# Expert down products of a mixture-of-experts block on one Trainium2 core: three float32r products of halves instead of one float32 product

## The chip, the cores and the metric

The kernel runs on 1 core of one Trainium2 chip. The metric is the device time of one launch in microseconds (us). Lower is better.

## The reference

The input `x` (2 sequences of 512 tokens, 256 wide) is normalised, and two branches are added to it: 16 heads of causal attention, and a block with a second attention (16 query and 4 key heads, rotary) that is followed by a mixture of 32 experts. The part that the change touches is the last product of an expert, `hmid` times `wed`:

```
probs = jax.nn.softmax(router_logits, axis=-1)
_, sel = jax.lax.top_k(probs + bias_e, K)            # K = 4 of E = 32 experts
...
g = jnp.einsum('th,ehi->tei', xf, weg)               # 256 -> 128
u = jnp.einsum('th,ehi->tei', xf, weu)               # 256 -> 128
hmid = jax.nn.silu(g) * u * cw[:, :, None]
moe_y = jnp.einsum('tei,eih->th', hmid, wed)         # 128 -> 256
shared = jax.nn.silu(xn @ wsg) * (xn @ wsu) @ wsd
return resid2 + moe_y + shared
```

## The kernel before

One program for the five engines, with semaphores written out by hand; each engine has its own instruction list, and nothing reorders it. The work runs in 64 units (16 heads x 2 sequences of the rotary attention, then as many of the plain one), one per window `n`. In window `n` TensorE (PE) computes the scores of unit n+1, turns and applies the probabilities of unit n, and projects the queries and keys of unit n+2.

Precision: most products are sums of three float32r products. A float32 value is split in a part `hi` (the value written as float32r) and `lo = value - hi`; `mm3` multiplies hi*hi, hi*lo and lo*hi (`PASSES`). One engine, mostly ScalarE (ACT), writes `hi`, and VectorE (DVE) writes `lo`.

The experts' tokens are sorted into 63 blocks of 128 slots, two blocks to a pair, pairs 4 to 35 (pairs 0 to 3 are the shared expert). Windows 45 to 60 carry two pairs each as "guests" between the pieces of the attention. Per pair there are three chunks:

- `X`: PE turns the rows `xb`; ACT evicts them to `xbT`.
- `G`: gate and up products; ACT makes tanh (L1257), DVE makes the silu (L1721) and the product with up (L1731), into `hb`. `hb`, `xbT` and the expert weights `w0`, `w1`, `w2` lie in one big tensor, which the profile calls `late`.
- `Y`: the down product, L971, `hb` times the down weights `wdn`, a float32 matmul of 128x256 per block. ACT scales it (L1273), and GpSimd (POOL) scatters it with an indirect DMA (L757).

On PE the order inside such a window is (function `step`): scores 0 and 1 of the next unit (L995, L868), X, a V projection, X, output projection, turn of the probabilities (L1010), scores 2, G, scores 3, G, Q projection, K projection, `attend` (nine L868 and L1026), Y (L971), turn, Y, turn.

ACT and DVE follow: for each of Q and K, ACT writes `hi` (L1233) and DVE then a plain copy of 128 columns (L1511) and `lo` (L1512); then ACT and DVE do the same for the attention's output `zT` (L1210, L1486). DVE takes the inverse row sums (L1464) in between. POOL multiplies the probabilities with them (L695), sends the scatters and, in some windows, splits attention weights of a later group of heads (`weights`: `hi` at L681, `lo` at L685). Those weight jobs come last in POOL's list for a window; in windows 45 to 60 there is one each in 45, 46, 47, 48, 50, 53, 54, 55, 56 and 58, and two in 52.

Q, K, V, O, X, G and Y share four PSUM banks in turn; `taken` semaphores count when a bank has been read.

Of the kernel before, what the change touches and what calls it, by code (L numbers as in the profile page):

```python
# [5 lines left out]
def attention_pair_moe_kernel(  # L6
# [38 lines left out]
    P = 128  # L45
# [176 lines left out]
    with ctx:  # L222
        def sb(name, cols, dt=f32, rows=P):
            return ctx.enter_context(nc.sbuf_tensor(name, [rows, cols], dt))
# [20 lines left out]
        ro_t = sb("raw_o", 2 * 2 * D)  # L245
        mask_t = sb("mask", S)
        ident = sb("ident", P)
        rows_t = sb("const_rows", P)
        cols_t = sb("const_cols", 64)
        gate_keep = sb("gate_cols", KD * E)  # L250
        bO_t = sb("b_o", D)
        be_t = sb("bias_e", E)
        nmax_t = sb("neg_max", 2 * TB)
        sum_t = sb("row_sum", 2 * TB)
# [16 lines left out]


        with ExitStack() as early:
            accA_t, xrT_t, rope_t, t1_t, sw_t, vt_t = (
                early.enter_context(nc.sbuf_tensor(name, [P, cols], dt)) for name, cols, dt in (
                    ("acc_a", NT * D, f32), ("xrT", 2 * KD * NT * P, f32r), ("rope", 2 * S, f32),
                    ("rope_sum", 3 * S, f32), ("rope_swapped", 2 * S, f32), ("vT", S, f32)))
        PW = 2 * KD * 2 * P + 2 * D
        late_t = sb("late", 2 * PW + 4 * P + 4 * ROW + KD * NT * P + KD * 2 * P + D + NT * ROW)
        idx_t = sb("dest", NT * TOPK, i32)  # L280
        et_t = sb("block_expert", 2 * (PAIRS - SHARED))
        ei_t = sb("block_expert_int", 2 * (PAIRS - SHARED), i32)
# [4 lines left out]
            return late_t[:, took[0] - cols:took[0]]  # L287

        w0_t, w1_t, hb_t, xb_t = late(PW), late(PW), late(4 * P), late(4 * ROW)
        x2T_t, ws_t, rows_t2 = late(KD * NT * P), late(KD * 2 * P + D), late(NT * ROW)  # L290
        w2_t = rows_t2[:, 0:PW]

        x_slots = nc.dram_tensor("x_slots_dram", [SLOTS, ROW], f32)
# [49 lines left out]
        wdn = [w[:, GU:GU + 2 * D].rearrange("p (j d) -> p j d", j=2) for w in (w0_t, w1_t, w2_t)]  # L343
        sgu = ws_t[:, 0:KD * 2 * P].rearrange("p (k c) -> p k c", k=KD)
        sdn = ws_t[:, KD * 2 * P:]
        cws = cws_t[:, :].rearrange("p (s j) -> p s j", s=4)
        cwj = cwj_t[:, :].rearrange("p (h s j k) -> p h s j k", h=2, s=2, j=2)
        ids = ids_t[:, :].rearrange("p (s j) -> p s j", s=4)
# [56 lines left out]
        wr_in = [sem(f"w_pair_in{i}") for i in range(3)]  # L405
        et_out, et_in = sem("blocks_stored"), sem("blocks_loaded")
        th_done, s_done, meta = sem("tanh_done"), sem("silu_done"), sem("slot_meta")
        y_out = [sem("y_scattered0"), sem("y_scattered1")]
        waits_passed = sem("waits_passed")
        acc_done0, out_sem = sem("moe_added_first"), sem("out_written")  # L410
# [426 lines left out]
        def _(pe):  # L837
# [77 lines left out]
            def guest(ch):  # L915
                kind = ch[0]
                dst = bR[BANK[ch]]
                vacant(pe, ch)
                if kind == "T2":
                    b, k = ch[1] // KD, ch[1] % KD  # L920
                    for t in range(TB):
                        pe.wait_ge(rows_scaled, b * TB + t + 1)
                        m = pe.transpose(dst[:, t * P:(t + 1) * P], x2r[:, b * TB + t, k * P:(k + 1) * P], ident[:, :])
                elif kind == "L":
                    kept(pe, ("T2", 3))
                    for t in range(NT):
                        for k in range(KD):
                            m = pe.matmul(dst[:, t * E:(t + 1) * E], x2T[:, k, t * P:(t + 1) * P],
                                          gate_keep[:, k * E:(k + 1) * E], start=t == 0 and k == 0,
                                          stop=t == NT - 1 and k == KD - 1, skip_group_check=True)  # L930
                elif kind == "R":
                    pe.wait_ge(masked, 1)
                    pe.wait_ge(ones_done, 4)
                    chosen = route[:, 2, :, 0:E]
                    pe.matmul(dst[:, 0:NT * E], before_t, chosen, start=True, stop=False, skip_group_check=True)
                    for t in range(1, NT + 1):
                        m = pe.matmul(dst[:, t * E:(NT + 1) * E], ones_t, chosen[:, 0:NT + 1 - t, :], start=False,
                                      stop=t == NT, skip_group_check=True)
                elif kind == "X":
                    r = ch[1]  # L940
                    pe.wait_ge(xs_in[r % 2], 16 * ((r - SHARED) // 2 + 1))
                    for k in range(KD):
                        for j in blocks_of(r):
                            m = pe.transpose(dst[:, (k * 2 + j) * P:(k * 2 + j + 1) * P],  # L944
                                             xb[:, r % 2, j, k * P:(k + 1) * P], ident[:, :])
                elif kind == "G":
                    r = ch[1]
                    if r < SHARED:
                        pe.wait_ge(sh_in, 48)
                    else:  # L950
                        pe.wait_ge(wr_in[(r - SHARED) % 3], 96 * ((r - SHARED) // 3) + 48 * len(blocks_of(r)))
                        kept(pe, ("X", r))
                    if r < SHARED:
                        for w in range(2):
                            for k in range(KD):
                                m = pe.matmul(dst[:, w * 2 * P:(w + 1) * 2 * P], sgu[:, k, w * P:(w + 1) * P],
                                              x2T[:, k, 2 * r * P:(2 * r + 2) * P], start=w == 0 and k == 0,
                                              stop=w == 1 and k == KD - 1, skip_group_check=True)
                    else:
                        for w in range(2):  # L960
                            for j in blocks_of(r):
                                for k in range(KD):
                                    m = pe.matmul(dst[:, (2 * w + j) * P:(2 * w + j + 1) * P],  # L963
                                                  wgu[(r - SHARED) % 3][:, j, k, w * P:(w + 1) * P],
                                                  xbT[:, r % 2, k, j * P:(j + 1) * P], start=w == 0 and j == 0 and k == 0,
                                                  stop=w == 1 and j == blocks_of(r)[-1] and k == KD - 1, skip_group_check=True)
                else:
                    r = ch[1]
                    kept(pe, ("G", r))
                    for j in blocks_of(r):  # L970
                        m = pe.matmul(dst[:, j * D:(j + 1) * D], hb[:, r % 2, j, :],  # L971
                                      sdn if r < SHARED else wdn[(r - SHARED) % 3][:, j, :], start=j == 0,
                                      stop=j == blocks_of(r)[-1],
                                      skip_group_check=True)
                m.then_inc(j_mm, 1)

            def guests(n, *slots):
# [170 lines left out]
        def _(act):  # L1148
# [128 lines left out]
            def guests(n, *slots):  # L1277
                for slot in slots:
                    for ch in guests_of(n, slot):
                        guest(ch)  # L1280

            def scale_rows(tiles):

                for t in tiles:
                    act.wait_ge(ln_pow, B + 1 + t // TB + 1)
                    act.wait_ge(rp_lo["Qrope"], HALF)
                    act.activation(x2r[:, t, 0:D], accA[:, t, :], ACT.Identity,
                                   scale=rstd[:, 2, t:t + 1]).then_inc(rows_scaled, 1)
# [10 lines left out]
            def step(n, it):  # L1299
# [21 lines left out]
                if not rotary:  # L1321
# [8 lines left out]
                    probs_hi(n, 2, it)  # L1330
                    scale_rows(SCALED.get((n, 0), ()))
                    normalise(n, (0, 1))
                    if nxt:
                        exp(n + 1, 2, it)
                    guests(n, 3)
# [1 line left out]
                        exp(n + 1, 3, it)  # L1337
                    guests(n, 4)
                    normalise(n, (2,))
                    for ch in chs[:2]:  # L1340
                        chunk_a(ch, it)
                    normalise(n, (3,))
                    if n == LOGITS:
                        act.wait_ge(shifted, 1)
# [38 lines left out]
        def _(ve):  # L1383
# [181 lines left out]
            def step(n, it):  # L1565
# [33 lines left out]
                if not rotary:  # L1599
# [14 lines left out]
                    if nxt:  # L1614
                        mask_scores(n + 1, 3, it)
                    times_up(n, 3)
                    if nxt:
                        invert(n + 1, 2, it)
                    silu(n, 4)
                    if nxt:  # L1620
                        invert(n + 1, 3, it)
                    times_up(n, 4)
                    guests(n, 4)
                    route_m(n)
                    for ch in chs[:2]:
                        chunk(ch, it)
                    z_part(n, it)
                    route_1(n)
                    guests(n, 5, 6)
# [94 lines left out]
            def times_up(n, slot):  # L1724

                for ch in guests_of(n, slot):
                    if ch[0] == "G":
                        r = ch[1]
                        both = bR[BANK[ch]][:, :].rearrange("p (w j c) -> p w j c", w=2, j=2)
                        ve.wait_ge(s_done, r + 1)  # L1730
                        ve.tensor_tensor(hb[:, r % 2], both[:, 1], hb[:, r % 2],  # L1731
                                         ALU.mult).then_inc(taken[BANK[ch]], 1)

            fetched = [0]

# [162 lines left out]
```

## Time and profile before

| | |
|---|---|
| median of 3 runs | 773.32 us (771.32 to 773.82) |
| time of the profiled execution | 773.67 us |
| its span, first to last instruction | 771.8 us |
| mean granted TensorE clock | 0.990 |
| PE busy | 745.4 us, 97% |
| DVE, ACT, POOL busy | 547.1, 488.8, 478.1 us |

Window 54 of the program, used below as the example, lies at 625 to 641.4 us in the span, counted from one Y to the next. The stretch with expert pairs, windows 45 to 60, goes from about 477 to 741 us. "A x4" in a timeline row is four merged instructions; a float32 matmul leaves two matmul records, a float32r matmul one. Consecutive instructions of one engine overlap a little in the records (DVE by 0.08 us).

### The profile page before, as it was taken

How to read it: one execution, taken by the hardware profiler on the slowest of the kernel's cores; microseconds unless marked ns; L12 is line 12 of the kernel's file. 1: busy time of each engine (PE TensorE's matmuls, PEld its weight loads, DVE VectorE, ACT ScalarE, POOL GpSimd, SP SyncE). 2: the span in 40 equal slices, each digit the busy share in tenths (PEclk: the TensorE clock that was granted, in tenths of full speed). 3: DMA queues.
4: the chain of work that ended last, by engine and by line, in shares of the span. 5: the costliest groups of instructions: out<-in, count | busy, mean ns of one | idle time of the engine just before them, and what ended most of it. 6: DMA issues, size and time to landing. Idle time of an engine off the chain costs nothing. (4 is left out here: it accounts for less than half of the span.)

```text
span 771.8 us, 14397 instructions
## 1 busy us (share of the span) xinstructions
PE 745.4 (97%) x4641; PEld 663.2 (86%) x4641; DVE 547.1 (71%) x1687; ACT 488.8 (63%) x1218; POOL 478.1 (62%) x553
## 2 busy tenths in 40 slices
PE   7789899999999999999989999999999999999997
PEld 4578788888889899888878889999999999999986
DVE  5888888887979787766688667655556565555574
ACT  2677677787778776568354665655566565566652
POOL 5658577777867696335363774466564766656553
PEclk8999999999999999999999999999999999999999
DMA  6000000100011079700101462476877777667634
GB/s 194 8 15 28 14 15 15 35 15 22 15 42 42 15 227 278 187 14 15 42 15 47 101 201 84 98 177 162 202 177 166 182 177 171 145 156 168 126 56 142
DMA packets 102691, 76.99 MB, mean 100 GB/s; under 512 B 6918, under 2 KB 101466, under 8 KB 102618
## 3 DMA queue, kind: packets, MB, share of 16 engines
q1 hardware_dynamic: 91426, 62.74, 28.6%
q0 software_dynamic: 10608, 12.61, 10.3%
q8 instruction: 38, 0.62, 0.3%
q10 hardware_dynamic: 584, 0.73, 0.3%
q14 instruction: 35, 0.29, 0.1%
HBM read 51.36 MB, written 24.69 MB: 99 GB/s over the span
## 5 line engine op out<-in xcount | busy, mean ns | idle before, releaser
L695 POOL TENSOR_SCALAR probs<-probs,inv_sum 128x128 f32<-128x128 f32 x240 | 141.2, 604 | 152.7 <-DVE inv_sum L1464 147.5
L1185 ACT ACTIVATE probs<-probs,neg_max 128x128 f32<-128x128 f32 (+3 forms) x256 | 143.0, 559 | 121.6 <-DVE neg_max L1458 120.3
L868 PE MATMUL s<-k_heads,q_heads 128*128 128x256 f32 (+2 forms) x576 | 138.8, 362 | 3.3 <-DVE neg_max L1458 3.0
L1458 DVE CUSTOM_DVE_ANT_0 probs<-s,mask 128x128 f32<-128x128 f32 (+3 forms) x256 | 120.0, 485 | 16.7 <-PE s L868 10.7
L757 POOL DMA_INDIRECT moe_sum_dram<-late,slot_tokens x63 | 99.2, 1574 | 38.2 <-ACT late L1273 26.5
L1473 DVE TENSOR_TENSOR probsT<-t,probsT 128x384 fp32r<-128x384 f32 (+2 forms) x192 | 101.2, 548 | 12.9 <-ACT probsT L1200 12.5
L1200 ACT ACTIVATE probsT<-t 128x384 fp32r<-128x384 f32 (+2 forms) x192 | 90.1, 488 | 18.5 <-PE t L1010 18.3
L868 PEld LDWEIGHTS s<-k_heads,q_heads 128*128 128x128 f32 x576 | 91.2, 190 | 9.6 <-DVE neg_max L1458 5.9
L1010 PE MATMUL t<-ident,probs 128*128 128x128 f32 x640 | 94.5, 274 | 3.1 <-POOL probs L695 2.3
L1010 PEld LDWEIGHTS t<-ident,probs 128*128 128x128 f32 x640 | 74.8, 140 | 12.6 <-POOL probs L695 4.4
L868 PE MATMUL zb<-probsT,v_heads 128*128 128x512 f32 (+2 forms) x351 | 68.9, 340 | 1.4 <-DVE probsT L1473 0.9
L868 PEld LDWEIGHTS zb<-probsT,v_heads 128*128 128x128 f32 x351 | 59.9, 188 | 8.8 <-DVE probsT L1473 1.4
L766 POOL TENSOR_TENSOR rope_swapped<-rope_swapped,rope 128x512 f32<-128x512 f32 x32 | 42.0, 1312 | 35.6 <-ACT rope_swapped L1226 35.6
L1464 DVE RECIPROCAL inv_sum<-row_sum 128x1 f32<-128x1 f32 x256 | 35.9, 156 | 32.3 <-ACT probs L1185 32.2
L868 PE MATMUL ob<-w_o,zT 128*128 128x256 f32 x408 | 56.8, 283 | 1.1 <-DVE xnT L1517 1.1
L868 PEld LDWEIGHTS ob<-w_o,zT 128*128 128x128 f32 x408 | 53.9, 190 | 4.0 <-DVE xnT L1517 1.3
L868 PE MATMUL j<-xrT,w_qk 128*128 128x512 f32 x192 | 52.4, 408 | 0.3 <-DVE rope_sum L1505 0.3
L1185 ACT ACTIVATION_READ_ACCUMULATOR probs<-probs,neg_max 128x1 f32 x256 | 47.9, 187 | 0.0
L772 POOL TENSOR_TENSOR q_heads<-rope_sum,q_heads 128x384 fp32r<-128x384 f32 x32 | 38.5, 1202 | 12.5 <-ACT q_heads L1296 10.7
L868 PE MATMUL j<-xnT,w_qk 128*128 128x512 f32 x174 | 45.2, 402 | 0.0
L868 PEld LDWEIGHTS j<-xrT,w_qk 128*128 128x128 f32 x192 | 34.0, 190 | 6.4 <-DVE rope_sum L1505 0.7
L706 POOL DMA_INDIRECT x_slots_dram<-late,dest x32 | 31.2, 975 | 12.1 <-issue 9.0
(258 smaller groups left out, 1592.2 us busy)
## 6 DMA issues: line engine op xcount, KB each, us to landing
x_slots_dram<-mask SPq DMA_DIRECT2D x1, 8480.0 KB, 38.1
late<-x_slots_dram SPq DMA_DIRECT2D x32, 265.0 KB, 4.4
late<-in_L_ffn_weg_dram SPq DMA_DIRECT2D x63, 128.0 KB
late<-in_L_ffn_weu_dram SPq DMA_DIRECT2D x63, 128.0 KB
late<-in_L_ffn_wed_dram SPq DMA_DIRECT2D x63, 128.0 KB
moe_sum_dram<-mask SPq DMA_DIRECT2D x2, 1152.0 KB, 8.2
raw_qk<-in_L_ffn_wq_dram SPq DMA_DIRECT2D x16, 128.0 KB, 2.2
raw_o<-in_L_ffn_wo_dram SPq DMA_DIRECT2D x8, 256.0 KB, 2.7
```

The source lines that it names most:

```text
L695: pool.tensor_scalar(piece, piece, rinv[:, u % 2, i:i + 1], 1.0, ALU.mult, ALU.mult).then_inc(p_norm, 1)
L706: pool.indirect_dma_start(out=x_slots[:, :], out_offset=bass.IndirectOffsetOnAxis(ap=idx[:, t, k:k + 1], axis=0), in_=x2r[:, t, :], in_off ...
L757: pool.indirect_dma_start(out=moe_sum[j][:, :], out_offset=bass.IndirectOffsetOnAxis(ap=ids[:, r % 4, j:j + 1], axis=0), in_=yb[:, r % 2, ...
L766: pool.tensor_tensor(swapped[kind], swapped[kind], sinT, ALU.mult).then_inc(rp_sin[kind], 1)
L772: pool.tensor_tensor(qT[:, v % 2, 1], rot_sum((kind, v))[:, P:S], qT[:, v % 2, 0].bitcast(f32), ALU.subtract).then_inc(rp_lo[kind], 1)
L868: m = pe.matmul(dst, lhs(a), rhs(b), start=first and i == 0, stop=last_ and i == 2, skip_group_check=skip)
L1010: m = pe.transpose(bT[at % 2][:, (j - lo_) * P:(j - lo_ + 1) * P], pr[:, u % 2, P_OFF[qt] + kt * P:P_OFF[qt] + (kt + 1) * P], ident[:, :])
L1185: act.activation(piece, piece, ACT.Exp, bias=nmax[:, u % 2, i:i + 1], scale=-1.0, accum_out=rsum[:, u % 2, i:i + 1]).then_inc(e_done, 1)
L1200: act.activation(pT[:, 0, (first - 1) * P:(b - 1) * P], bT[(3 * u + c) % 2][:, (first - a) * P:(b - a) * P], ACT.Copy).then_inc(pt_hi, 1)
L1458: ve.tensor_tensor_reduce(pr[:, u % 2, P_OFF[i]:P_OFF[i] + width], bS[i % 2][:, 0:width], mask_t[:, S - width:S], INV_SCALE, BIG, ALU.add, ...
L1464: ve.reciprocal(rinv[:, u % 2, i:i + 1], rsum[:, u % 2, i:i + 1]).then_inc(r_done, 1)
L1473: ve.tensor_tensor(pT[:, 1, cs], bT[(3 * u + c) % 2][:, (first - a) * P:(b - a) * P], pT[:, 0, cs].bitcast(f32), ALU.subtract).then_inc(pt ...
```

## The change

1. `Y` of the expert pairs becomes `mm3` on halves: `hs` (hi and lo of `hb` for two pairs) and `ds` (hi and lo of the down weights for two pairs). It waits for two new semaphores, `dn_lo` and `h_lo`, instead of `kept("G", r)`. The shared expert's Y stays float32.
2. ACT gets three instructions of 128x512 per window: `down_hi` for each pair, and `inner_hi` for both pairs together, behind the K chunk.
3. DVE gets three subtractions of 128x512 per window: `down_lo` for each pair, `inner_lo` for both together, behind the K chunk and ahead of `zT`. All of their inputs lie in SBUF.
4. The space: the shared expert's weights leave `late` for a tensor of their own, in whose place `hs` and `ds` lie afterwards (`down_hi` waits for the last shared Y). The constants `rows_t` and `bO_t` move to space that is reused later.

```diff
-        late_t = sb("late", 2 * PW + 4 * P + 4 * ROW + KD * NT * P + KD * 2 * P + D + NT * ROW)
+        late_t = sb("late", 2 * PW + 4 * P + 4 * ROW + KD * NT * P + NT * ROW)
+        with ExitStack() as shared:
+            ws_t = shared.enter_context(nc.sbuf_tensor("w_shared", [P, KD * 2 * P + D], f32))
+        hs_t, ds_t = sb("h_halves", 2 * 4 * P, f32r), sb("w_down_halves", 2 * 4 * D, f32r)
...
-                else:
+                elif ch[1] < SHARED:
                     r = ch[1]
                     kept(pe, ("G", r))
...
+                else:
+                    r = ch[1]
+                    pe.wait_ge(dn_lo, r - SHARED + 1)
+                    pe.wait_ge(h_lo, (r - SHARED) // 2 + 1)
+                    for j in blocks_of(r):
+                        m = mm3(dst[:, j * D:(j + 1) * D], lambda p: hs[:, p, r % 2, j, :],
+                                lambda p: ds[:, p, r % 2, j * D:(j + 1) * D], j == 0, j == blocks_of(r)[-1], skip=True)
...
+            def down_hi(n, i):
+
+                for r in pairs_of(n)[i:i + 1]:
+                    if r >= SHARED:
+                        act.wait_ge(wr_in[(r - SHARED) % 3], 96 * ((r - SHARED) // 3) + 48 * len(blocks_of(r)))
+                        act.wait_ge(j_mm, CHUNK["Y", max(r - 2, SHARED - 1)] + 1)
+                        act.activation(ds[:, 0, r % 2, :], wdn[(r - SHARED) % 3].rearrange("p j d -> p (j d)"),
+                                       ACT.Copy).then_inc(dn_hi, 1)
+
+            def inner_hi(n):
+
+                rs = pairs_of(n)
+                if rs and rs[0] >= SHARED:
+                    kept(act, ("G", rs[0]))
+                    kept(act, ("G", rs[1]))
+                    act.activation(hs_t[:, 0:4 * P], hb_t, ACT.Copy).then_inc(h_hi, 1)
...
                     normalise(n, (2,))
+                    down_hi(n, 1)
                     for ch in chs[:2]:
                         chunk_a(ch, it)
+                    inner_hi(n)
...
                     times_up(n, 4)
+                    down_lo(n, 1)
                     guests(n, 4)
                     route_m(n)
                     for ch in chs[:2]:
                         chunk(ch, it)
+                    inner_lo(n)
                     z_part(n, it)
...
+            def down_lo(n, i):
+
+                for r in pairs_of(n)[i:i + 1]:
+                    if r >= SHARED:
+                        ve.wait_ge(dn_hi, r - SHARED + 1)
+                        ve.tensor_tensor(ds[:, 1, r % 2, :], wdn[(r - SHARED) % 3].rearrange("p j d -> p (j d)"),
+                                         ds[:, 0, r % 2, :].bitcast(f32), ALU.subtract).then_inc(dn_lo, 1)
+
+            def inner_lo(n):
+
+                rs = pairs_of(n)
+                if rs and rs[0] >= SHARED:
+                    ve.wait_ge(h_hi, (rs[0] - SHARED) // 2 + 1)
+                    ve.tensor_tensor(hs_t[:, 4 * P:], hb_t, hs_t[:, 0:4 * P].bitcast(f32), ALU.subtract).then_inc(h_lo, 1)
```

The other new `down_hi(n, 0)` stands on ACT between the third turned piece of the probabilities and the exponential of scores 2, `down_lo(n, 0)` on DVE between the first `times_up` and an inverse.

DVE in window 54, before, from the first pair's product with up (L1731) to the first turned probabilities of the next unit:

```order
L1731 TENSOR_TENSOR late<-j0,late 128x256
L1464 RECIPROCAL inv_sum<-row_sum 128x1
L1721 SCALAR_TENSOR_TENSOR late<-late,j1 128x256
L1464 RECIPROCAL inv_sum<-row_sum 128x1
L1731 TENSOR_TENSOR late<-j1,late 128x256
L1511 TENSOR_SCALAR q_first<-ob,const_cols 128x128
L1512 SCALAR_TENSOR_TENSOR q_heads<-ob,const_cols,q_heads 128x384
L1511 TENSOR_SCALAR k_first<-zb,const_cols 128x128
L1512 SCALAR_TENSOR_TENSOR k_heads<-zb,const_cols,k_heads 128x512
L1486 SCALAR_TENSOR_TENSOR zT<-j0,const_cols,zT 128x512
```

The same place after the change:

```order
L1764 TENSOR_TENSOR late<-j0,late 128x256
L1772 TENSOR_TENSOR w_down_halves<-late,w_down_halves 128x512
L1494 RECIPROCAL inv_sum<-row_sum 128x1
L1754 SCALAR_TENSOR_TENSOR late<-late,j1 128x256
L1494 RECIPROCAL inv_sum<-row_sum 128x1
L1764 TENSOR_TENSOR late<-j1,late 128x256
L1772 TENSOR_TENSOR w_down_halves<-late,w_down_halves 128x512
L1541 TENSOR_SCALAR q_first<-ob,const_cols 128x128
L1542 SCALAR_TENSOR_TENSOR q_heads<-ob,const_cols,q_heads 128x384
L1541 TENSOR_SCALAR k_first<-zb,const_cols 128x128
L1542 SCALAR_TENSOR_TENSOR k_heads<-zb,const_cols,k_heads 128x512
L1780 TENSOR_TENSOR h_halves<-late,h_halves 128x512
```

Two subtractions of down weights come in (L1772), and one of `hb` (L1780) between the K chunk and `zT`, which follows it.

PE in window 54, before, around the two Y chunks:

```order
L868 MATMUL j0<-probsT,v_heads 128x256 x3
L1026 MATMUL j0<-probsT_last,v_last 128x128
L971 MATMUL j1<-late 128x256 x2
L1010 MATMUL t1<-ident,probs 128x128 x4
L971 MATMUL ob<-late 128x256 x2
```

PE after:

```order
L873 MATMUL j0<-probsT,v_heads 128x256 x3
L1036 MATMUL j0<-probsT_last,v_last 128x128
L873 MATMUL j1<-w_down_halves,h_halves 128x256 x6
L1020 MATMUL t1<-ident,probs 128x128 x4
L873 MATMUL ob<-w_down_halves,h_halves 128x256 x6
```

Each Y has six float32r matmuls where it had two float32 ones, in the same place: right behind the last matmul of `attend`. The lists of POOL and SyncE are the same but for the name of the shared weights' tensor.

## Rows read from the trace of the kernel before

**Rows 1.** The page: busy time per engine, and TensorE's clock in 40 slices.

```profile
PE 745.4 (97%) x4641; PEld 663.2 (86%) x4641; DVE 547.1 (71%) x1687; ACT 488.8 (63%) x1218; POOL 478.1 (62%) x553
PEclk8999999999999999999999999999999999999999
```

**Rows 2.** Busy time in two windows: span, then busy us of each engine.

```profile
core 0: us, PE busy (x) PEld busy (x) DVE busy (x) ACT busy (x) POOL busy (x), PEclk, DMA share, GB/s
624.97:641.42 16.45, 16.45 (x111) 15.08 (x111) 9.74 (x31) 9.88 (x25) 11.55 (x13) 1.00 0.76 165
```

**Rows 3.** Chain that ended last: start us, us, engine, tile, line, count.

```profile
624.97 0.87 PE ob L971 x4
...
639.63 1.57 PE j L868 x9
641.42 0.87 PE j L971 x4
...
642.73 0.86 PE ob L971 x4
...
646.87 1.44 PE ob L868 x12
```

**Rows 4.** Timeline of ACT, window 54: start us, us, instruction, idle time before.

```profile
633.94 0.62 ACT L1185 ACTIVATE probs<-probs,neg_max 128x384 f32<-128x384 f32 x1 [1.28 <-DVE neg_max L1458]
...
636.90 0.38 ACT L1257 ACTIVATE late<-j 128x256 f32<-128x256 f32 x1
638.28 0.58 ACT L1233 ACTIVATE q_heads<-ob,const_cols 128x384 fp32r<-128x384 f32 x1 [1.00 <-PE ob L868]
639.67 0.69 ACT L1233 ACTIVATE k_heads<-zb,const_cols 128x512 fp32r<-128x512 f32 x1 [0.80 <-PE zb L868]
641.46 0.69 ACT L1210 ACTIVATE zT<-j,const_cols 128x512 fp32r<-128x512 f32 x1 [1.10 <-PE j L1026]
```

**Rows 5.** Timeline of DVE, window 54.

```profile
637.77 0.42 DVE L1731 TENSOR_TENSOR late<-j,late 128x256 f32<-128x256 f32 x1
638.90 0.35 DVE L1511 TENSOR_SCALAR q_first<-ob,const_cols 128x128 f32<-128x128 f32 x1 [0.70 <-ACT q_heads L1233]
...
640.66 0.74 DVE L1512 SCALAR_TENSOR_TENSOR k_heads<-zb,const_cols,k_heads 128x512 fp32r<-128x512 f32 x1
642.18 0.75 DVE L1486 SCALAR_TENSOR_TENSOR zT<-j,const_cols,zT 128x512 fp32r<-128x512 f32 x1 [0.78 <-ACT zT L1210]
```

**Rows 6.** The nearest instructions to the added ones: min/median/max ns.

```profile
L1296 ACT ACTIVATE k_heads<-rope_sum x8: 616/620/632, 19.7 to 270.5; 128x512 fp32r<-128x512 f32 x8
L1536 DVE TENSOR_TENSOR k_heads<-rope_sum,k_heads x8: 677/678/1526, 21.6 to 272.1; 128x512 fp32r<-128x512 f32 x8
```

**Rows 7.** Chain near the end, where PE waits for DVE.

```profile
754.39 0.04 issue
754.43 1.86 PE ob L868 x9
```

**Rows 8.** POOL and DVE at one time, POOL first.

```profile
133.35 1.00 POOL L772 TENSOR_TENSOR q_heads<-rope_sum,q_heads 128x384 fp32r<-128x384 f32 x1
133.38 1.53 DVE L1536 TENSOR_TENSOR k_heads<-rope_sum,k_heads 128x512 fp32r<-128x512 f32 x1
```

**Rows 9.** POOL in windows 54, 46, 58 and 53, with DVE's K chunk of 46.

```profile
637.91 0.69 POOL L695 TENSOR_SCALAR probs<-probs,inv_sum 128x512 f32<-128x512 f32 x1 [0.83 <-DVE inv_sum L1464]
...
641.08 1.27 POOL L685 TENSOR_TENSOR w_qk<-raw_qk,w_qk 128x512 fp32r<-128x512 f32 x1
...
508.72 0.74 DVE L1512 SCALAR_TENSOR_TENSOR k_heads<-zb,const_cols,k_heads 128x512 fp32r<-128x512 f32 x1
509.16 1.27 POOL L685 TENSOR_TENSOR w_qk<-raw_qk,w_qk 128x512 fp32r<-128x512 f32 x1
...
706.87 1.27 POOL L685 TENSOR_TENSOR w_o<-raw_o,w_o 128x512 fp32r<-128x512 f32 x1
...
624.68 1.15 POOL L681 TENSOR_SCALAR w_qk<-raw_qk 128x512 fp32r<-128x512 f32 x1
```

More of the change, by code:

```diff
@@ L247, in attention_pair_moe_kernel @@
         ident = sb("ident", P)
-        rows_t = sb("const_rows", P)
         cols_t = sb("const_cols", 64)
         gate_keep = sb("gate_cols", KD * E)
-        bO_t = sb("b_o", D)
         be_t = sb("bias_e", E)
@@ L273, in attention_pair_moe_kernel @@
         with ExitStack() as early:
-            accA_t, xrT_t, rope_t, t1_t, sw_t, vt_t = (
+            accA_t, xrT_t, rope_t, t1_t, sw_t, vt_t, rows_t, bO_t = (
                 early.enter_context(nc.sbuf_tensor(name, [P, cols], dt)) for name, cols, dt in (
                     ("acc_a", NT * D, f32), ("xrT", 2 * KD * NT * P, f32r), ("rope", 2 * S, f32),
-                    ("rope_sum", 3 * S, f32), ("rope_swapped", 2 * S, f32), ("vT", S, f32)))
+                    ("rope_sum", 3 * S, f32), ("rope_swapped", 2 * S, f32), ("vT", S, f32),
+                    ("const_rows", P, f32), ("b_o", D, f32)))
         PW = 2 * KD * 2 * P + 2 * D
-        late_t = sb("late", 2 * PW + 4 * P + 4 * ROW + KD * NT * P + KD * 2 * P + D + NT * ROW)
+        late_t = sb("late", 2 * PW + 4 * P + 4 * ROW + KD * NT * P + NT * ROW)
+        with ExitStack() as shared:
+            ws_t = shared.enter_context(nc.sbuf_tensor("w_shared", [P, KD * 2 * P + D], f32))
+        hs_t, ds_t = sb("h_halves", 2 * 4 * P, f32r), sb("w_down_halves", 2 * 4 * D, f32r)
         idx_t = sb("dest", NT * TOPK, i32)
@@ L289, in attention_pair_moe_kernel @@
         w0_t, w1_t, hb_t, xb_t = late(PW), late(PW), late(4 * P), late(4 * ROW)
-        x2T_t, ws_t, rows_t2 = late(KD * NT * P), late(KD * 2 * P + D), late(NT * ROW)
+        x2T_t, rows_t2 = late(KD * NT * P), late(NT * ROW)
         w2_t = rows_t2[:, 0:PW]
@@ L345, in attention_pair_moe_kernel @@
         sdn = ws_t[:, KD * 2 * P:]
+        hs = hs_t[:, :].rearrange("p (w s j c) -> p w s j c", w=2, s=2, j=2)
+        ds = ds_t[:, :].rearrange("p (w s c) -> p w s c", w=2, s=2)
         cws = cws_t[:, :].rearrange("p (s j) -> p s j", s=4)
@@ L407, in attention_pair_moe_kernel @@
         th_done, s_done, meta = sem("tanh_done"), sem("silu_done"), sem("slot_meta")
+        dn_hi, dn_lo, h_hi, h_lo = sem("w_down_hi"), sem("w_down_lo"), sem("h_hi"), sem("h_lo")
         y_out = [sem("y_scattered0"), sem("y_scattered1")]
@@ L970, in guest @@
                     for j in blocks_of(r):
[L971 to L974, printed above, removed]
+                        m = pe.matmul(dst[:, j * D:(j + 1) * D], hb[:, r % 2, j, :], sdn, start=j == 0,
+                                      stop=j == blocks_of(r)[-1], skip_group_check=True)
+                else:
[5 more added lines that the diff above has]
+                                lambda p: ds[:, p, r % 2, j * D:(j + 1) * D], j == 0, j == blocks_of(r)[-1], skip=True)
                 m.then_inc(j_mm, 1)
@@ L1332, in step @@
                     normalise(n, (0, 1))
+                    down_hi(n, 0)
                     if nxt:
@@ L1616, in step @@
                     times_up(n, 3)
+                    down_lo(n, 0)
                     if nxt:
```

## The prediction

> **What bounds the kernel now.** I read the page first. PE is busy for 97% of the span, and its clock was granted in full but for the first slice [rows 1]. DVE and ACT are far below that. Then I looked at one window of the stretch with expert pairs, since the change touches nothing else: from one Y to the next it lasts 16.45 us, of which PE is busy 16.45 us and DVE and ACT 9.7 and 9.9 us [rows 2]. The chain of waits says the same: there it is PE alone, one group of matmuls behind the other [rows 3]. So whatever PE saves in these 16 windows comes off the span one to one, and whatever PE is made to wait is added one to one. Idle time of DVE and ACT (6.6 us of each window) would hold the added work many times over, but its sum decides nothing. What decides is whether the last of the added instructions is done when PE reaches Y. So the third view is the timeline of ACT and DVE around Y [rows 4, 5].
>
> **What PE saves.** In the chain, the Y of a pair with two blocks takes 0.87 us for four records of two float32 matmuls, 0.435 us a block [rows 3]. The float32r form has a row of the same shape: twelve 128x256 matmuls of the output projection take 1.44 us, 0.12 us each [rows 3]. Three of them are 0.36 us. The saving is 0.075 us a block, and 63 blocks make 4.7 us, 0.3 us in a window with two pairs. This is the whole of what can be won.
>
> **What ACT adds.** Three 128x512 copies, SBUF to SBUF, float32r out. The same form took 0.62 us [rows 6]. The first (down weights) stands before the exponential of scores 2, where ACT was idle for 1.28 us; the second before the Q chunk, behind tanh, which ends at 637.28, where it was idle for 1.00 us [rows 4]. Both fit: cost nothing, and if that cover were gone 0.62 us each of lateness in ACT's list, not yet in PE's. The third (`hb`) can only start when the K chunk's `hi` ends, at 640.36, and ends by about 640.95. The zT eviction behind it starts at 641.46 [rows 4], so it isn't late either. ACT adds nothing to PE's path by itself.
>
> **What DVE adds.** Three 128x512 subtractions with both inputs in SBUF. The same form took 0.68 us in the median [rows 6]. The first delays an inverse by 0.6 us; POOL needs that for its third product, and the fourth one, which waits for a later inverse, starts at 637.91 as before [rows 9], so turned probabilities are not late. The second comes in behind the product with up, which ends at 638.19; DVE was idle 0.70 us before the Q chunk at 638.90 [rows 5]. It fits by a few hundredths, and a little lateness there is taken up before the K chunk. Cost nothing.
>
> The third is the one that PE waits for. It stands behind the K chunk's `lo`, which ends at 641.40 [rows 5]; with DVE's usual overlap of 0.08 it starts at 641.32 and ends at 642.00. Before, Y needed no more than `hb`, which was complete at 638.19; PE came to Y at 641.42, when `attend` ended [rows 3]. Now the operand is ready 0.58 us after PE is. What is queued behind the waiting PE is everything: the turn of the next unit, the other Y, the next window. What a restart costs on PE is shown once, near the end: an "issue" of 0.04 us after DVE's end and then 1.86 us for nine matmuls of `attend` [rows 7] that take 1.57 us without a wait [rows 3], so 0.29 us more (the first weight load and the array's fill are no longer hidden). The stall is 642.00 + 0.04 + 0.29 - 641.42 = 0.91 us. It recurs in each of the 16 windows, since each timing in it (K chunk on ACT, on DVE, `attend` on PE) hangs on PE's own K projection, which moves along: 16 x 0.91 = 14.6 us. Nothing after it wins it back, because PE has no other idle time there.
>
> **The port.** Does the third subtraction really take 0.68 us? Its inputs are both in SBUF, and POOL works at the same moment. The trace has one instruction of exactly this form that started just behind one of POOL: POOL ran from 133.35 to 134.35, DVE started at 133.38 and took 1.53 us instead of 0.68, to 134.91, which is 0.56 us after POOL's end [rows 8]. DVE seems to have stood still until POOL was done. DVE's K chunk, which has one input in PSUM, took the usual 0.74 us beside POOL's work [rows 5, 9], so before the change nothing in these windows showed it. That is what the Trainium skill says in "SBUF — State Buffer", section "Who interferes with whom": a DVE instruction with two SBUF inputs and a GpSimd instruction that reads SBUF exclude each other, and the later one waits for the whole of the earlier. By that rule, the trace agrees with the row of 1.53 us, and the sum gets the term that follows; without the rule and the row it would end without it.
>
> In window 54 POOL's weight job holds from 641.08 to 642.35 [rows 9]. The subtraction wants to start at 641.32, so it would end at 642.35 + 0.56 = 642.91 instead of 642.00: 0.91 us more. I went through the 16 windows for POOL's job at the end of DVE's K chunk: in 46, 47, 48, 54, 55, 56 and 58 it lies as in 54 (46 and 58 are shown; in 46 POOL started at 509.16, and DVE's K chunk ended at 509.46 [rows 9]). In 53 it is the job's other half, at 624.68 for 1.15 us [rows 9], 0.1 us shorter in effect. In 45 the job is over by then, in 52 it comes later, in 50 the two start within some hundredths of each other, which I count as none, and 49, 51, 57, 59 and 60 have no job. Eight windows x 0.89 = 7.1 us. The row that shows the exclusion has another POOL instruction, a subtraction too; the bounds of this term are 0 (no exclusion here) and 8.0 (window 50 as well).
>
> **Moved memory.** The tensors moved change no instruction's place or size; SyncE's and POOL's lists are the same. `down_hi` waits in ACT's list for the expert weights, which PE needs for G earlier than that (the copy comes behind the third turned piece in ACT's list, G ahead of it on PE); and for a Y of the window before. Nothing, between 0 and some tenths in the first window.
>
> **The sum**, against the profiled execution's own 773.67 us (span 771.8 us, the rest lies around it): 773.7 - 4.7 + 14.6 + 7.1 = 790.7 us. The profiled execution lies 0.35 us above the median of the runs shown (773.32), which is nothing here. About 0.3%, 2.3 us, is what a measurement of this kernel can tell from no change.
>
> **Rivals.**
> - *The port is not contended here:* DVE gets through in 0.68 us, or POOL's jobs lie elsewhere in the changed program. For it: one row shows the exclusion by POOL, not hundreds, and both sides' starts are some tenths apart. Against it: that row has exactly the added form. 773.7 - 4.7 + 14.6 = 783.6 us.
> - *The halves are hidden, faster:* the subtraction of `hb` ends before PE needs it. PE must have it 0.33 us ahead of 641.42 to lose nothing, at 641.09; it comes at 642.00. It decides at 0.91 us: if the added subtraction and the K chunk on DVE took that much less together (they take 1.0 and 0.68), or `attend` that much more. Then only the saving is left: 773.7 - 4.7 = 769.0 us. For it speaks only that 6.6 us of a window are idle on DVE; the order in DVE's list speaks against it.
> - *Half of it:* the restart costs less than 0.29 us, since a Y's first matmul is shorter than that of `attend`, and PE waits 0.62 us a window: 773.7 - 4.7 + 9.9 = 778.9 us, without the port.
> - *More of it:* POOL's scatters hold DVE up as well, or the second subtraction meets POOL's fourth product (637.91 for 0.69 us [rows 9]), ends at 639.16 and pushes Q and with it K. That uses the idle time before K in DVE's list; if K were pushed by 0.3 us in all windows, 4.8 us more: 795.5 us.
>
> **How the numbers follow.** Forecast with the port, 787 to 793 us: 0.52. Port free, 781 to 786 us: 0.20. More of it, 793 to 800 us: 0.11. Half of it, 776 to 781 us: 0.09. Hidden, 769 us: 0.06. Within 0.3%: 0.02. The range from 779.0 to 796.0 us takes in the first two, most of the third and some of the fourth, 0.84 together. Faster 0.06, same 0.02, slower 0.92.
>
> **What the changed profile would show.** PE gets idle time before the first Y of each of the 16 windows, with the subtraction of `h_halves` on DVE as the releaser: 16 times, two sizes, near 0.6 and 1.5 us by the timeline. The second Y of a window has none. Six records of Y take 0.72 us in the chain. The subtraction of `h_halves` lasts 0.68 us in eight windows and about 1.6 us in the other eight, where POOL's weight job (L681, L685) had started first; the subtractions of the down weights have idle time before the Q chunk to end in. I am wrong if PE stays busy through, if the idle time lies elsewhere, or if the subtraction has one length in all windows.

## The result, and the profile after

| | before | after |
|---|---|---|
| median | 772.35 us (771.32 to 773.82, 4 runs) | 782.21 us (781.66 to 783.17, 4 runs) |
| profiled execution, span | 773.67, 771.8 us | 781.66, 779.8 us |
| PE, DVE, ACT, POOL busy | 745.4, 547.1, 488.8, 478.1 us | 742.2, 580.6, 512.4, 488.0 us |

The change makes the kernel slower: ratio 1.0131, 95% interval 1.0106 to 1.0157, or 9.9 us by the medians (the ratios here and below come with the measurement and are not quotients of the medians). I had forecast 790.7 us, within 779 to 796. The time is in the range, but it is the time of a rival (port not contended, 783.6 us), not of the forecast.

The page of after shows where it goes in one line, against [rows 1]: PE is busy 3 us less, in a longer span.

```profile
PE 742.2 (95%) x4704; PEld 663.6 (85%) x4704; DVE 580.6 (74%) x1735; ACT 512.4 (66%) x1266; POOL 488.0 (63%) x553
```

One window lasted 16.45 us before with PE busy throughout [rows 2]. In after it lasts 17.10 us; PE is busy for 16.38 of them (a stretch of one window's length; columns: stretch, its length, then busy us of each engine).

```profile
627.57:644.67 17.10, 16.38 (x115) 15.16 (x114) 11.78 (x35) 11.36 (x28) 11.14 (x11) 1.00 0.68 156
```

All of PE's waits between 485 and 750 us have one releaser, the subtraction of `h_halves` (columns: who waited, for whom, us in total, times, longest). There are 16 of them, one per window, 11.6 us together:

```profile
PE j L873 <- DVE h_halves L1780: 5.8, 8, 0.7
PE zb L873 <- DVE h_halves L1780: 2.9, 4, 0.8
PE ob L873 <- DVE h_halves L1780: 2.9, 4, 0.7
```

The chain of waits of after, window 54 (start us, us, what), is the counterpart of [rows 3]. Where the chain stayed on PE through `attend` into Y, it now leaves PE when the K projection ends, goes through ACT's K, DVE's K and the added subtraction, and comes back for Y:

```profile
641.51 1.40 PE zb L873 x6
642.90 0.02 issue
642.92 0.70 ACT k_heads L1243
643.62 0.03 issue
643.65 0.35 DVE k_first L1541
644.00 0.66 DVE k_heads L1542
644.66 0.61 DVE h_halves L1780
645.27 0.14 issue
645.40 0.95 PE j L873 x6
646.35 0.44 PE t L1020 x4
646.79 0.71 PE ob L873 x6
```

From the end of K (642.90) to the start of Y is 2.50 us. `attend` takes 1.79 us in [rows 3], 639.63 to 641.42. The difference is PE's idle time. The second Y takes 0.71 us where it took 0.87 us before; the first has the restart in it, 0.95 us.

I compare stretches by the start of the scores of units 46 and 62, which bound windows 45 to 60. From one to the other it took 262.0 us before and 272.3 us after (479.03 to 741.01, and 476.74 to 748.99). The stretch explains 10.3 us, a little more than the medians differ. One of the 16 windows, 53, lasts 16.79 us before and not 16.45: ACT evicted that window's `xbT` late, behind a wait for the DMA of a scatter, and PE's weight load for G waited for it. First ACT's wait, then PE's (PEld is PE's weight load), both before:

```profile
612.55 0.47 ACT L1273 ACTIVATE late<-j,slot_weights 128x256 f32<-128x256 f32 x1 [1.69 <-DMA moe_sum_dram<-late,slot_tokens]
...
615.81 1.86 PEld L963 LDWEIGHTS j<-late 128*128 128x128 f32 x16 [0.32 <-ACT late L1264]
```

After lacks this wait. So a usual window is 0.65 us longer than before, and window 53 only 0.32 us.

Up to the stretch, the profiled execution of after was 2.3 us ahead of that of before: 0.7 us of it came in the first 53 us, and 1.6 us where the clock of the profiled before fell to half for a while. The PEclk column (third from the right) says 0.50, which is the 1.2 GHz level, and 1.00 in after, which is 2.4 GHz. So my reading of [rows 1], full clock but for the first slice, was too coarse: a 9 there stands for 90% or more of a slice. First before, then after:

```profile
372.00:374.00 2.00, 2.00 (x6) 1.57 (x5) 0.00 (x0) 0.58 (x1) 1.38 (x2) 0.50 0.00 0
```

```profile
372.00:374.00 2.00, 2.00 (x11) 1.73 (x10) 1.09 (x3) 1.22 (x3) 0.76 (x1) 1.00 0.04 11
```

I don't put that down to the change: of the seven kernels below, which all have the added work, four show this gain in this place and three don't. The profiled before, on which I based the sum, simply lay at the slow end of its runs.

The timelines of DVE and POOL in window 54 of after differ from what I had worked out. First DVE, then POOL (start us, us):

```profile
641.03 0.42 DVE L1764 TENSOR_TENSOR late<-j,late 128x256 f32<-128x256 f32 x1
641.37 1.03 DVE L1772 TENSOR_TENSOR w_down_halves<-late,w_down_halves 128x512 fp32r<-128x512 f32 x1
642.32 0.34 DVE L1541 TENSOR_SCALAR q_first<-ob,const_cols 128x128 f32<-128x128 f32 x1
643.92 0.74 DVE L1542 SCALAR_TENSOR_TENSOR k_heads<-zb,const_cols,k_heads 128x512 fp32r<-128x512 f32 x1
644.58 0.68 DVE L1780 TENSOR_TENSOR h_halves<-late,h_halves 128x512 fp32r<-128x512 f32 x1
```

```profile
641.16 0.70 POOL L700 TENSOR_SCALAR probs<-probs,inv_sum 128x512 f32<-128x512 f32 x1 [0.22 <-DVE inv_sum L1494]
...
642.01 1.83 POOL L762 DMA_INDIRECT moe_sum_dram<-late,slot_tokens  x1
...
644.59 1.80 POOL L690 TENSOR_TENSOR w_qk<-raw_qk,w_qk 128x512 fp32r<-128x512 f32 x1
```

Three pairs matter here. The second subtraction of down weights started 0.21 us behind POOL's fourth product, lasted 1.03 us, not 0.68, and ended 0.54 us after the product. POOL's scatter, which then started while that subtraction ran, lasted 1.83 us, not 1.57. And POOL's weight job started 0.01 us *behind* the subtraction of `h_halves`; before, it started 0.32 us ahead of the end of DVE's K chunk [rows 5, 9]. So the subtraction took 0.68 us and POOL's job had to wait, 1.80 us instead of 1.27. All 16 subtractions of `h_halves` last 0.68 or 0.69 us, and in all nine windows where this half of a job is near, POOL starts 0.01 to 0.04 us behind.

### The profile page after: what moved, and what is told of

It is laid out like the page before. It is cut to its first block, busy times and chain, and to the rows that moved or that the text cites. A ratio compares the mean times of both kernels' runs of the same rounds, so it can differ in the third digit from the quotient of the medians.

```text
span 779.8 us, 14667 instructions
## 1 busy us (share of the span) xinstructions
PE 742.2 (95%) x4704; PEld 663.6 (85%) x4704; DVE 580.6 (74%) x1735; ACT 512.4 (66%) x1266; POOL 488.0 (63%) x553
## 4 chain that ended last, share of the span: by engine, by line
PE 37%; DVE 8%; ACT 4%; issue 1%; DVEq 0%
PE j L873 9%; PE ob L873 5%; PE zb L873 5%; PE s L873 4%; PE j L968 4%; PE t L1020 3%; PE zb L968 2%; PE ob L968 2%; DVE k_heads L1542 2%; ACT k_heads L1243 1%; DVE h_halves L1780 1%; ACT probs L1195 1%; PE j L949 1%; DVE probsT L1503 1%; DVE k_first L1541 1%
## 5 line engine op out<-in xcount | busy, mean ns | idle before, releaser
L762 POOL DMA_INDIRECT moe_sum_dram<-late,slot_tokens x63 | 103.0, 1635 | 42.8 <-ACT late L1283 31.5
L1494 DVE RECIPROCAL inv_sum<-row_sum 128x1 f32<-128x1 f32 x256 | 36.0, 156 | 32.2 <-ACT probs L1195 32.2
L1502 DVE COPY probsT_last<-t 128x128 f32<-128x128 f32 x64 | 18.3, 285 | 33.0 <-ACT probsT L1210 32.9
```

Source lines behind the costliest of these rows:

```text
L762: pool.indirect_dma_start(out=moe_sum[j][:, :], out_offset=bass.IndirectOffsetOnAxis(ap=ids[:, r % 4, j:j + 1], axis=0), in_=yb[:, r % 2, ...
L1494: ve.reciprocal(rinv[:, u % 2, i:i + 1], rsum[:, u % 2, i:i + 1]).then_inc(r_done, 1)
```

## The experiments

Four of the runs were made on one chip, where before had a median of 772.6 us: those of the first three sections, and "Both down weights early". The other three ("A real delay", "The second down weights behind Q", "The wait without the saving") were made on another, where before had 798.4 us. Their profiles lose 24 to 28 us ahead of the stretch, at 440 to 476 us, with waits for most of which they name no releaser. Of before there is no profile from that chip, but its time is as much longer. I read those three by their difference to before on the same chip, and by the stretch from unit 46 to unit 62, which holds the windows in question. A window without a job of POOL's lasts 17.10 us in after on the first chip and in "The second down weights behind Q" on the other (49, 51, 57, 59), so stretches from the two chips can be compared.

### Same work, nobody waits for the last of it

```diff
-                    pe.wait_ge(h_lo, (r - SHARED) // 2 + 1)
+                    kept(pe, ("G", r))
...
-                        m = mm3(dst[:, j * D:(j + 1) * D], lambda p: hs[:, p, r % 2, j, :],
-                                lambda p: ds[:, p, r % 2, j * D:(j + 1) * D], j == 0, j == blocks_of(r)[-1], skip=True)
+                        m = pe.matmul(dst[:, j * D:(j + 1) * D], hb[:, r % 2, j, :], wdn[(r - SHARED) % 3][:, j, :], ...)
```

> The changed kernel's work on ACT and DVE in the same places, but Y is a float32 product of hb and the down weights again; it waits for the halves of the down weights and for hb, not for the halves of hb, and nothing reads the halves. Chain theory: all the added work on ACT and DVE is hidden when PE does not wait for the last of it, so the time is that of the kernel before, 772.4 us, within 1 us. Rival (the added work costs by itself, by the port or by lateness of zT, Q or K): 774 us or more.

Measured: 771.3 us, ratio to before 1.0002 (0.9985 to 1.0019). In 15 of the 16 windows the profile runs at before's pace to 0.01 us; window 53 is 0.35 us shorter, since before's wait there is missing. PE has no wait in the whole stretch. So the added 48 instructions on ACT and 48 on DVE cost nothing by themselves in these places, with their contention, by which POOL's job takes 1.60 to 1.81 us in nine windows here too. The rival that the load on DVE or the port costs falls.

### The halves of `hb` between Q and K

```diff
-                    for ch in chs[:2]:
+                    for ch in chs[:1]:
                         chunk_a(ch, it)
                     inner_hi(n)
+                    for ch in chs[1:2]:
+                        chunk_a(ch, it)
...
-                    for ch in chs[:2]:
+                    for ch in chs[:1]:
                         chunk(ch, it)
                     inner_lo(n)
+                    for ch in chs[1:2]:
+                        chunk(ch, it)
```

> The changed kernel with both halves of hb made between the Q chunk and the K chunk, on ACT and on DVE, instead of behind the K chunk. Chain theory (PE's idle time before the first Y is only the subtraction's place at the end of ACT's and DVE's list): the subtraction ends near 0.7 us after the Q chunk, more than 1 us ahead of Y; PE's 16 idle times vanish and only the saving is left: 782.2 - 16 x 0.65 - 4.7 + 0 = 767.1 us taken from the changed kernel's median, 772.35 - 4.7 = 767.7 us from the kernel before. Rival (the added work itself loads DVE or the port so much that something else is late, K's lo by the subtraction, or the scores behind it): PE keeps idle time, now before the scores of the next unit, 772 us or more.

Measured: 769.84 us, against 772.59 us for before; ratio 0.9969 (0.9947 to 0.9991). This version is faster than both kernels, against before by 0.3%. I had expected 767.1 to 767.7 us, some 2 us less. Its DVE and PE in window 54:

```profile
637.76 0.68 DVE L1784 TENSOR_TENSOR h_halves<-late,h_halves 128x512 fp32r<-128x512 f32 x1
638.37 0.34 DVE L1543 TENSOR_SCALAR k_first<-zb,const_cols 128x128 f32<-128x128 f32 x1
```

```profile
639.09 0.96 PE L873 MATMUL j<-w_down_halves,h_halves 128*128 128x256 f32 x6
```

The subtraction ends at 638.44, 0.65 us ahead of Y, and PE goes straight on. Over the stretch it gains 3.9 us on before, against 4.7 expected; a usual window gains 0.30 or 0.31 us, but windows 45 and 50 are 0.5 and 0.6 us longer than a usual one. In window 50 PE waits 0.4 us for the DMA of the rows `xb`. Window 45 shows the port (POOL, then DVE):

```profile
491.22 1.29 POOL L690 TENSOR_TENSOR w_qk<-raw_qk,w_qk 128x512 fp32r<-128x512 f32 x1
```

```profile
491.37 1.69 DVE L1784 TENSOR_TENSOR h_halves<-late,h_halves 128x512 fp32r<-128x512 f32 x1
```

Here POOL was first by 0.15 us, and the very instruction that the change adds stood still until POOL's end at 492.51 and ended 0.55 us after it, as in [rows 8]. In the other 15 windows it took 0.67 to 0.69 us.

### A hair of delay

```diff
+                    ve.memset(pad_t[:, :], 0.0)
                     ve.tensor_tensor(hs_t[:, 4 * P:], hb_t, hs_t[:, 0:4 * P].bitcast(f32), ALU.subtract)
```

> The changed kernel with one tiny DVE memset (128x8, about 0.1 us) ahead of the subtraction of h_halves. In the changed kernel's trace that subtraction starts 0.01 to 0.04 us before POOL's weight job (L690) in 9 windows. Port theory (an exclusive shared read port, decided by who starts first): POOL now comes first in those 9 windows, the subtraction lasts 1.7 to 1.9 us instead of 0.68, PE waits about 1.2 us more in each, and 0.1 us more in the others: 782.2 + 9 x 1.2 + 7 x 0.1 = 793.7 us, in the range 790 to 796. Rival (no port contention, the length of 0.68 is the instruction's own): 16 x 0.1 = 1.6 us more, 783.8 us, and all 16 subtractions at 0.68 us.

Measured: 782.8 us, ratio 1.0149 (1.0118 to 1.0179), with all 16 subtractions at 0.68 us. These are the signs that I had given for the rival, but they say nothing on the port, since the order did not change as intended. The memset was hidden in its neighbours' overlap and moved the subtraction by 0.01 us, not 0.1 us. POOL's job and the subtraction then started within 0.01 us of each other in most windows, sometimes POOL by the record the earlier one, and still it was POOL that waited (1.82 us) and DVE that took 0.68 us. The recorded starts don't tell who wins a tie of 0.01 us.

### A real delay

```diff
+                    ve.tensor_reduce(pad_t[:, 0:1], mask_t[:, 0:2 * P], AX.X, ALU.max)
                     ve.tensor_tensor(hs_t[:, 4 * P:], hb_t, hs_t[:, 0:4 * P].bitcast(f32), ALU.subtract)
```

> The changed kernel with one DVE maximum over 256 columns of the mask (result unused, one SBUF input) ahead of the subtraction of h_halves, in place of the memset, which hid itself: with it the subtraction began only 0.01 us later. A reduction of this size took 0.42 us in the trace of the kernel before, about 0.33 net of overlap. POOL's weight job starts 0.01 us behind the subtraction's old start, so it now starts some 0.3 us ahead of it in 9 windows. Port theory: there the subtraction ends 0.55 us after POOL's end, lasts about 1.5 us, and PE waits about 0.8 us more on top of the 0.33: 782.2 + 16 x 0.33 + 9 x 0.8 = 794.7 us, in the range 792 to 797. Rival (order does not decide, the subtraction always takes 0.68): 782.2 + 5.3 = 787.5 us.

Measured: 828.56 us against 798.38 us, ratio 1.038 (1.0332 to 1.0428), 30.2 us over before; the stretch takes 29.2 us more than before's, 19.0 us more than after's, which makes 801.2 us out of after's 782.2, above my range of 792 to 797. DVE and POOL in window 54:

```profile
679.01 0.41 DVE L1781 TENSOR_REDUCE pad<-mask 128x1 f32<-128x256 f32 x1
679.33 1.50 DVE L1782 TENSOR_TENSOR h_halves<-late,h_halves 128x512 fp32r<-128x512 f32 x1
```

```profile
679.02 1.26 POOL L691 TENSOR_TENSOR w_qk<-raw_qk,w_qk 128x512 fp32r<-128x512 f32 x1
```

In 8 windows the subtraction lasts 1.49 to 1.52 us, in the others 0.68 to 0.71 us. By windows, against after's 0.655 us over before: windows with a free port 0.97 us (0.32 us more, as expected), windows with POOL first 1.80 us (another 0.83 us, as expected 0.8). So the rival, that the order does not matter, is out. The rest I had not expected. Window 53 has a subtraction of 0.70 us and yet a PE wait of 1.9 us, 0.9 us more than I can put down to the delay. There ACT's eviction of a Y waited for the DMA of a scatter, and the chain of waits runs from it to the K chunk on DVE, which came that much later:

```profile
648.52 0.48 ACT L1284 ACTIVATE late<-j,slot_weights 128x256 f32<-128x256 f32 x1 [1.50 <-DMA moe_sum_dram<-late,slot_tokens]
```

Windows 47, 48, 49 and 55, 56, 57 are another 0.8 to 1.3 us longer each, 6.3 us in all. In them the clock fell four times to 0.50, the 1.2 GHz level, for 3.4 us each, which can cost 6.8 us at most (4 x 3.4 us at half speed). The first time is behind PE's wait of 1.9 us in window 47, the second such wait in a row; the stretch ahead has 1.00:

```profile
548.00:552.40 4.40, 2.61 (x15) 2.18 (x13) 3.93 (x8) 1.95 (x4) 3.69 (x3) 1.00 0.26 30
553.30:556.70 3.40, 3.40 (x19) 3.40 (x17) 0.75 (x2) 2.44 (x6) 1.82 (x2) 0.50 0.39 113
```

16 x 0.32 + 8 x 0.83 + 0.9 + 6.3 = 19.0 us, as measured.

### Both down weights early

```diff
                     down_hi(n, 0)
+                    down_hi(n, 1)
...
-                    down_hi(n, 1)
...
                     down_lo(n, 0)
+                    down_lo(n, 1)
...
-                    down_lo(n, 1)
```

> The changed kernel with the second pair's halves of the down weights made right behind the first pair's, on ACT and DVE. In the changed kernel the second subtraction of down weights waits for POOL's fourth product, lasts 1.02 us and overlaps the start of POOL's scatter, which lasts 1.83 us instead of 1.57 and so pushes POOL's weight job from 0.32 us before to 0.07 us before the end of DVE's K chunk, just behind the start of the subtraction of h_halves. Theory (that push is what kept my port term of 7 us from coming): without it the scatter lasts 1.57 us again, the weight job starts some tenths ahead of the subtraction of h_halves in 8 or 9 windows, the subtraction lasts 1.6 to 1.9 us there, and the time is 782.2 + 8.5 x 1.0 = 790.7 us, in the range 788 to 793. Rival (the job's place has another cause): 782 us, with all subtractions of h_halves at 0.68 us.

Measured: 782.87 us, ratio 1.0146 (1.0105 to 1.0186). The expectation is missed, because the experiment did something else besides. The scatter lasted 1.58 us, as expected. But two subtractions in a row ahead of an inverse (L1494) made POOL's third product wait for it, and all that follows on POOL came more than a microsecond later in the window. The weight job's second half then started behind the subtraction of `h_halves` or during it, and the subtraction had mixed lengths (0.68 to 1.05 us). So the run neither shows nor refutes the theory of the push. Of the port it shows one more case: in window 53 the first half of the job started 0.74 us ahead of the subtraction, which lasted 0.96 us and ended 0.55 us after it (POOL, then DVE):

```profile
626.92 1.15 POOL L686 TENSOR_SCALAR w_qk<-raw_qk 128x512 fp32r<-128x512 f32 x1
```

```profile
627.66 0.96 DVE L1780 TENSOR_TENSOR h_halves<-late,h_halves 128x512 fp32r<-128x512 f32 x1
```

In windows 54, 55, 56 and 58 the first half started 0.10 to 0.26 us ahead while a scatter still ran, and both got longer: 0.89 to 1.05 us for the subtraction, 1.61 us for the half of the job. Order alone does not give that; it stays open.

### The second down weights behind Q

```diff
                     times_up(n, 4)
-                    down_lo(n, 1)
...
-                    for ch in chs[:2]:
+                    for ch in chs[:1]:
                         chunk(ch, it)
+                    down_lo(n, 1)
+                    for ch in chs[1:2]:
+                        chunk(ch, it)
                     inner_lo(n)
```

> The changed kernel with the second subtraction of down weights on DVE moved behind the Q chunk (ACT's list is left alone), so that it no longer meets POOL's fourth product and the start of POOL's scatter. The run with both subtractions early could not test this, because it made POOL's products 1.2 us later. Theory (the scatter's 1.83 instead of 1.57 us is that subtraction's doing, and it moved POOL's weight job behind the subtraction of h_halves): the scatter lasts 1.57 us, the job starts about 0.3 us before the end of the K chunk on DVE, and in 8 windows the subtraction of h_halves lasts 1.5 to 1.7 us: 782.2 + 8 x 0.9 = 789.4 us, up to 791 with a K chunk some hundredths late. Rival (the job stays where it is): 782 to 783.5 us.

Measured: 818.63 us against 798.38 us, ratio 1.0247 (1.0212 to 1.0281), 20.2 us over before. The stretch takes 19.4 us more than before's, 9.2 us more than after's, which makes 791.4 us out of after's 782.2; I had expected 789.4 to 791. POOL and DVE in window 54:

```profile
674.69 1.57 POOL L762 DMA_INDIRECT moe_sum_dram<-late,slot_tokens  x1 [0.16 <-issue]
675.78 1.15 POOL L686 TENSOR_SCALAR w_qk<-raw_qk 128x512 fp32r<-128x512 f32 x1
677.01 1.26 POOL L690 TENSOR_TENSOR w_qk<-raw_qk,w_qk 128x512 fp32r<-128x512 f32 x1
```

```profile
676.60 0.74 DVE L1542 SCALAR_TENSOR_TENSOR k_heads<-zb,const_cols,k_heads 128x512 fp32r<-128x512 f32 x1
677.25 1.57 DVE L1782 TENSOR_TENSOR h_halves<-late,h_halves 128x512 fp32r<-128x512 f32 x1
```

The scatter is back at 1.57 us, the job starts at 677.01, 0.33 us ahead of the K chunk's end (677.34), and the subtraction lasts 1.57 us. It does so in nine windows: 46, 47, 48, 50, 53, 54, 55, 56 and 58; in 52 it lasts 0.87 us, in the others 0.68 us. Against after, eight of the nine windows are 0.87 to 0.91 us longer, and window 50 is 1.26 us longer, of which I count 0.9 as this: 8.0 us together. The rest of the 9.2 us lies elsewhere: 0.4 us more in window 50, where PE stood still once more, ahead of X; 0.6 us in 45, where the moved subtraction itself started behind POOL's job, lasted 1.42 us and made K late; and 0.2 us in 52. The port term of my forecast is there again, brought back by moving one hidden instruction by two places.

### The wait without the saving

The float32 Y of the first experiment, but with the changed kernel's two waits.

> The changed kernel with all added work and both new waits, but Y as a float32 product of hb and the down weights; the halves are made and waited for, and not read. Chain theory: the time is the changed kernel's plus the saving that I took from the chain of waits, 782.2 + 4.7 = 786.9 us (16 stalls of 0.95 us over the kernel before), in the range 785.5 to 788. Rival (the float32r product saves little or nothing here, since six weight loads stand against two): 782 to 784 us.

Measured: 814.47 us against 798.38 us, ratio 1.0185 (1.0144 to 1.0226), 16.1 us over before. The stretch takes 15.1 us more than before's and 4.8 us more than after's. By the stretch the saving is 4.8 us, as expected (787.0 us out of after's 782.2, where I had 786.9). The waits are worth 15.1 us against before. Against the first experiment's kernel, which lacks before's wait in window 53, they are worth 15.4 us (277.07 - 261.65), 0.96 us each.

## Why the prediction was right or wrong

1. **PE is the bound, and the rest is cover.** Right. Without the last wait the added work costs 0.0 us.
2. **The saving, 4.7 us.** Right: 4.8 us between the runs with and without it, and 0.30 us a window in the version that hides the halves.
3. **ACT hidden, first and second subtraction on DVE hidden.** Right in cost, not in size. The second subtraction was to take 0.68 us and fit "by a few hundredths"; it took 1.02 us in 15 of 16 windows, behind POOL's fourth product. DVE's idle time ahead of K took that up.
4. **The wait for the third subtraction, 14.6 us.** Right, slightly small: 15.1 us against before, 0.96 us a window where I had 0.91. The restart of PE after the wait costs 0.14 us of issue and 0.24 us in the first Y (0.95 against 0.71 us), 0.38 us together; I had 0.33 us.
5. **The port, 7.1 us.** This is the step that failed: in after it is 0. One of my own signs of being wrong came true, that the subtraction of `h_halves` has one length in all windows; and PE's waits have one size, 0.7 us, not two. The mechanism is there: in all 18 cases of three runs in which the second half of POOL's job starts 0.1 to 0.3 us ahead of it, the added instruction lasts 1.49 to 1.69 us and ends 0.54 to 0.55 us after POOL. What failed is that I took POOL's place in the window from the trace of before, and did not carry my own added instruction through to it. The second subtraction overlaps the start of POOL's scatter, which lasts 0.26 us longer, and so the job slips from 0.32 us to 0.07 us ahead of the K chunk's end, 0.01 us behind the start of the subtraction (0.08 us ahead of that end). The order flips, DVE goes first, and POOL, which has time, pays (1.80 for 1.27 us). Moving that one subtraction brings the term back: 8.0 us in nine windows, which is what I had as the bound with nine.
   I had said that the rule of the Trainium skill, "SBUF — State Buffer", section "Who interferes with whom", agrees with the row of 1.53 us. It holds in those 18 cases as well, to the clause that the order of starting decides, with one difference: the later one ends 0.55 us after the earlier, less than its own 0.68 us. It was I who got the order wrong. The four windows of "Both down weights early" in which both got longer it does not explain.
6. **The base.** 773.67 us for the profiled before was 1.3 us above the median of the four runs of the result.

The sum again, on the median and with measured terms: 772.35 - 4.8 + 15.1 + 0 = 782.6 us; measured 782.21 us. The forecast was 8.5 us too high: 7.1 us for the port and 1.3 us for the base. That the time still lies within 779 to 796 us is owed to the width of the range, which took in the rival without the port, at a chance of 0.20, and not to the forecast.

## What to carry to other kernels

Where one engine is busy all the time, an added instruction elsewhere costs what the chain to its consumer is longer than that engine's own work in between, however idle its engine is on average: 0.68 us put at the end of a list cost 15 us, and the same put one chunk earlier 0.5 us, in the one window where it met POOL's job. What two engines share by first come cannot be costed from the trace of before: each added instruction has to be carried through to both, since a shift of 0.3 us decided 8 us here. If a term hangs on an order that is closer than some tenths, both cases belong in the sum.

## What the runs showed that I had not expected

- A DVE subtraction with two SBUF inputs lengthens POOL's indirect-DMA instruction. In after, the 14 scatters that started while the second subtraction of a window ran took 1.82 to 1.85 us, and one that started while the first ran (window 52) 1.82 us; the other 48 had a median of 1.58 us. With the second subtraction elsewhere only the one in window 52 was left at 1.82 us, and all 63 had a median of 1.57 us.
- Whoever comes second does not pay its whole length after the first is done: the subtraction of 0.68 us ends 0.55 us after POOL's end, and POOL's job of 1.27 us ends 1.15 us after the subtraction's.
- In the run with the real delay, PE waited 1.9 us in windows 46 to 48, 50, 53 to 56 and 58. Behind the waits of 47, 48, 55 and 56 the granted clock was 0.50 for 3.4 us, behind the others it stayed at 1.00; six windows took 6.3 us more. In the run with the second down weights behind Q, with waits of 1.6 us in the same nine windows, and in after, with 0.7 us in every window, it was 1.00 throughout the stretch.
